# Segment-max pass of a four-layer graph network: the message transposes two chunks ahead, the scan one chunk ahead of the additions, three partial sums to a bank

## The reference, cut to what matters

```python
msgs = z[edge_dst] @ Wd + z[edge_src] @ Ws + edge_weight[:, None] * ww[None, :] + bm
agg = jax.ops.segment_max(msgs, edge_dst, num_segments=n)
...
agg = jnp.where(deg[:, None] > 0, agg, jnp.zeros((), dtype=z.dtype))
...
hidden = jax.nn.relu(z @ W1a + agg @ W1b + b1)
return hidden @ W2 + b2                      # then residual, layer norm, and the table of the last pass
```

## Time and profile before

| | |
|---|---|
| Median of 3 runs | 3425.28 us (3420.51 to 3431.15) |
| Profiled execution, span | 4033.3 us |
| Mean granted TensorE clock in it | 0.859 |
| Max pass in it (first to last scan) | 1997.7 to 3379.1 us |
| Busy share, whole span: PE, PEld, DVE, ACT, POOL | 80, 56, 42, 24, 59 % |

### The profile page before, as it was taken

One profiled execution on the slowest core, in us unless ns is written; L12 is line 12 of the kernel. 1 busy time (PEld: TensorE's weight loads), 2 busy tenths in 40 slices (PEclk: granted clock), 3 DMA queues, 4 the chain that ended last, 5 costly groups with the idle time before them and its releaser, 6 DMA issues.

```text
span 4033.3 us, 59669 instructions
## 1 busy us (share of the span) xinstructions
PE 3216.6 (80%) x22050; PEld 2272.7 (56%) x22050; DVE 1712.9 (42%) x3999; ACT 954.4 (24%) x2526; POOL 2364.2 (59%) x2341
## 2 busy tenths in 40 slices
PE   3688788788888888888677887777777786989898
PEld 2344444455557777776455665555665664545554
DVE  6465555132231222111355555555655564333333
ACT  2455455132230111011222222222222222000000
POOL 3766662666634666665255555655655562677775
PEclk6899999889999999998777678877877777999999
DMA  5444444656555666665432333333333335666564
GB/s 150 146 158 166 164 144 155 203 174 198 183 163 193 198 198 208 200 190 189 142 94 74 101 102 101 104 101 102 105 112 96 100 108 195 238 202 227 199 217 138
DMA packets 285336, 629.16 MB, mean 156 GB/s; under 512 B 60235, under 2 KB 194964, under 8 KB 277494
## 3 DMA queue, kind: packets, MB, share of 16 engines
q1 hardware_dynamic: 178038, 378.50, 27.5%
q0 software_dynamic: 105280, 245.39, 20.7%
q10 hardware_dynamic: 1728, 1.38, 0.1%
HBM read 480.93 MB, written 144.13 MB: 155 GB/s over the span
## 4 chain that ended last, share of the span: by engine, by line
PE 60%; issue 15%; another core or an unknown queue 8%; DVE 8%; ACT 6%; DMA 1%; DVEq 1%; SPq 0%; POOL 0%; ACTq 0%; POOLq 0%
PE banks L1777 25%; PE banks L1239 7%; PE banks L461 7%; PE banks L549 4%; PE banks L1798 3%; PE banks L1258 3%; PE banks L1796 3%; PE banks L1234 2%; PE banks L524 2%; PE banks L1893 1%; PE banks L1127 1%; ACT arena L2126 1%; DVE arena L488 1%; ACT arena L1409 1%
## 5 line engine op out<-in xcount | busy, mean ns | idle before, releaser
L1777 PE MATMUL banks<-arena 128*128 128x384 bf16 (+1 forms) x9310 | 1545.1, 315 | 123.8 <-issue 115.1
L1777 PEld LDWEIGHTS banks<-arena 128*128 128x128 bf16 x9310 | 910.6, 100 | 603.9 <-issue 218.4
L511 POOL DMA_INDIRECT arena<-tab_l,ring_of_rows x831 | 819.8, 986 | 615.6 <-PE banks L1239 330.6
L461 PE MATMUL banks<-arena 128*128 x1758 | 426.9, 352 | 321.1 <-issue 161.3
L1844 POOL DMA_INDIRECT arena<-h_pieces,span_sources x450 | 434.6, 966 | 315.0 <-issue 107.1
L1844 POOL DMA_INDIRECT ring_of_rows<-message_pieces,span_sources x396 | 429.4, 1084 | 227.2 <-issue 101.0
L461 PEld LDWEIGHTS banks<-arena 128*128 128x128 f32 x1758 | 331.7, 245 | 386.7 <-issue 385.4
L1822 DVE TENSOR_TENSOR arena<-iota_bf,span_targets 128x768 bf16<-128x768 bf16 x243 | 135.1, 557 | 837.1 <-remote 337.8
L488 DVE TENSOR_TENSOR arena<-arena,banks 128x129 f32 x879 | 251.6, 286 | 537.3 <-PE banks L461 337.9
L1844 POOL DMA_INDIRECT ring_of_rows<-x_pieces,span_sources x306 | 334.1, 1092 | 202.9 <-PE banks L1796 91.4
L1844 POOL DMA_INDIRECT ring_of_rows<-l_pieces,span_sources x306 | 300.0, 980 | 232.7 <-issue 71.9
(11 more groups left out here) (246 smaller groups left out, 3151.2 us busy)
## 6 DMA issues: line engine op xcount, KB each, us to landing
arena<-edge_counts SPq DMA_DIRECT2D x83, 896.0 KB
arena<-edge_counts SPq DMA_DIRECT2D x83, 672.0 KB
edge_counts<-arena SPq DMA_DIRECT2D x32, 1568.0 KB
typed_counts<-arena SPq DMA_DIRECT2D x27, 1568.0 KB
arena<-scan_mask SPq DMA_DIRECT2D x208, 128.0 KB
arena<-typed_counts SPq DMA_DIRECT2D x27, 896.0 KB
arena<-typed_counts SPq DMA_DIRECT2D x27, 672.0 KB
arena<-tab_l,ring_of_rows POOLq DMA_INDIRECT x831
```

Of the source, the lines that this page charges most:

```text
L461: T.matmul(place(s, k.bank[:n_banks], cols), k.OH[:, s % OH_RING, :], k.RG[:, bass.ds(base, cols)], start=True, stop=True).then_inc(p.prod ...
L511: k.nc.gpsimd.indirect_dma_start(k.RG3[:, i % p.ring, at:at + width], None, table, bass.IndirectOffsetOnAxis(ap=k.SRC[:, i:i + 1], axis=0) ...
L1777: t = T.matmul(k.bank[i % N_SUMS][:, 0:rows.shape[-1]], counts[:, s, :], rows, start=s == 0 and n == 0, stop=s == NT - 1 and n == len(term ...
```

## The change: what it does

It concerns the regular program's max pass.

- TensorE gets a function of its own, `max_tensor_l2`. Messages are turned two chunks ahead, alternately into banks 2 and 6. The order for chunk c is slot 0, `turn_messages(c + 2)`, slot 1, turn back c, slot 2, typed counts, slot 3.
- VectorE runs scan c + 1 ahead of chunk c's additions (`max_chunks`).
- Step results go three to a bank (`TRIPLE`, 136 columns each), still in banks 0 and 1. The lag of the additions stays at two steps (`MAX_LAG`). The first addition of three waits for all three products; products of a triple wait for the additions of the triple two before it.
- Masks and weight rows get a third buffer (`MASKS`).
- The dense part of a group uses one bank (`max_bank`) in place of four. The last projection and its bias addition are therefore done in two halves of two node tiles (`parts`, `table`, `parts2`, `table2`), which makes 21 stages of 19. The number of steps between stages (71 or 72 steps // stages) stays 3 for the full groups.
- Three semaphores are merged with others.

```diff
+MAX_LAG = 2
+TURNS_OF_MAX = (2, 6)
+MASKS = 3
+TRIPLE, TRIPLE_COLS = 3, 136
...
-    "l2": (*STAGES["l2"], *PIECES),
+    "l2": (*STAGES["l2"], "parts2", "table2", *PIECES),
...
+def max_bank(g):
+    return banks_of(g)[0]
+def max_tiles(g, half):
+    return gtiles(g)[2 * half:2 * half + 2]
...
+def max_place(k, s):
+    return k.bank[s // TRIPLE % 2][:, s % TRIPLE * TRIPLE_COLS:s % TRIPLE * TRIPLE_COLS + H + 1]
...
+    def step(s):
...
+        if s % OH_BATCH == 0:
+            T.wait_ge(p.hot, s // OH_BATCH + 1)
+        if s % TRIPLE == 0 and s >= 2 * TRIPLE:
+            T.wait_ge(p.added, s - TRIPLE)
+        if s == 0 or p.newest(s) // CH != p.newest(s - 1) // CH:
+            T.wait_ge(k.sem("l2_back_copied"), p.newest(s) // CH + 1)
+        T.matmul(max_place(k, s), k.OH[:, s % OH_RING, :], k.RG[:, bass.ds(base, H + 1)], start=True, stop=True).then_inc(p.product, 1)
...
+    def turn_messages(c):
+        tiles, bank = chunk_tiles(c), k.bank[TURNS_OF_MAX[c % 2]]
+        if c >= 2:
+            T.wait_ge(k.sem("l2_scanned"), c - 1)
...
+    turn_messages(0)
+    turn_messages(1)
+    T.wait_ge(k.sem("l2_acc_set"), 1)
+    for c in range(NCH):
+        steps(k.slots[c][0])
+        if c + 2 < NCH:
+            turn_messages(c + 2)
+        steps(k.slots[c][1])
+        turn_back(c)
+        steps(k.slots[c][2])
+        if typed_unit(c):
+            tensor_typed_counts(k, *typed_unit(c))
+        steps(k.slots[c][3])
...
+    def add(s):
+        if s % TRIPLE == 0:
+            V.wait_ge(p.product, min(s + TRIPLE, STEPS))
...
+    def scan(c):
+        n = len(chunk_tiles(c)) * P
+        V.wait_ge(k.sem("l2_turned"), c + 1)
+        V.wait_ge(k.sem(f"load_mask_{c % MASKS}"), 32 * (c // MASKS + 1))
+        if c >= 2:
+            V.wait_ge(k.sem("l2_back"), c - 1)
...
+    def max_chunks():
+        scan(0)
+        for c in range(NCH):
+            if c + 1 < NCH:
+                scan(c + 1)
+            for which in k.slots[c][0:3]:
+                steps(which)
...
```

More of the change, by code:

```diff
@@ L1227, in turn_messages @@
         tiles = chunk_tiles(c)
-        if not p.regular:
-            T.wait_ge(k.sem("l2_message"), tiles[-1] + 1)
+        T.wait_ge(k.sem("l2_message"), tiles[-1] + 1)
         if c:
             T.wait_ge(k.sem("l2_scanned"), c)
-        if p.regular:
-            T.wait_ge(k.sem(f"load_mask_{c % 2}"), 32 * (c // 2 + 1))
-            T.matmul(k.bank[TURN][:, 0:len(tiles) * P], k.WW9, k.W9[c % 2][:, 0:len(tiles) * P], start=True, stop=False)
         for q, i in enumerate(tiles):
[L1236 to L1241, removed]
+            t = T.transpose(k.bank[TURN][:, q * P:(q + 1) * P], k.RG3[:, i % p.ring, UP:UP + H], k.IDENT)
         t.then_inc(k.sem("l2_turned"), 1)
@@ L1292, in node @@
             vector_invert(k, p, g, stage)
+        elif stage in ("table", "table2") and p.regular:
+            half = stage == "table2"
+            if max_tiles(g, half):
+                V.wait_ge(*p.at("parts2" if half else "parts", g))
+                rows, n = wide(region(k.HT, g, H2), H2), len(max_tiles(g, half))
+                V.tensor_tensor(rows[:, 2 * half:2 * half + n, :], wide(k.bank[max_bank(g)][:, 0:n * H2], H2), spread(k.bdc, n, H2),
+                                ALU.add).then_inc(p.sem(stage), 1)
         elif stage == "table":
             V.wait_ge(*p.at("parts", g))
-            if before_group(g) >= 0 and not p.regular:
+            if before_group(g) >= 0:
                 V.wait_ge(*p.stored("l3", before_group(g)))
@@ L1311, in node, with max_step @@
             t.then_inc(p.sem(stage), 1)
+    def add(s):
+        if s % TRIPLE == 0:
+            V.wait_ge(p.product, min(s + TRIPLE, STEPS))
+        if s:
+            V.wait_ge(p.added, s)
+        if s % REGS == 0:
+            V.load(k.ve_regs, k.BASES[1:2, s:s + REGS])
+        dst = k.ACC[:, bass.ds(V.snap(k.ve_regs[s % REGS], min_val=0, max_val=(NT - 1) * SLOT), H + 1)]
+        V.tensor_tensor(dst, dst, max_place(k, s), ALU.add).then_inc(p.added, 1)
+    def max_step(s):
+        if s == 0:
+            vector_one_hots(k, p, 0, k.LOCEND)
+        if s % OH_BATCH == 0 and s + OH_BATCH < STEPS:
+            vector_one_hots(k, p, s + OH_BATCH, k.LOCEND)
+        if s >= MAX_LAG:
+            add(s - MAX_LAG)
@@ new lines, in max_chunks @@
+    def max_chunks():
[5 more added lines that the diff above has]
+                steps(which)
+            if typed_unit(c + 2) and c % 2 == 0:
+                vector_typed_one_hots(k, (c + 2 + UNITS) // 2)
+            if c in FIRST_TYPE_AT:
+                vector_first_type(k, Plan(k, "l3", True), 0, FIRST_TYPE_AT.index(c))
+            if c in FIRST_HOT_AT:
+                vector_rows_hot(k, Plan(k, "l3", True), FIRST_HOT_AT.index(c))
+            steps(k.slots[c][3])
+        steps(k.slots[NCH][0])
+        for s in range(STEPS - MAX_LAG, STEPS):
+            add(s)
+        for stage, g in p.tail:
+            node(stage, g)
@@ L1319, in message @@
     def message(i):
-        if i < N_ET and not p.regular:
+        if i < N_ET:
             V.wait_ge(*p.landed(i))
@@ L1470, in first_slab @@
         load_typed_slab(k, Plan(k, "l3", True), 0, h)
-    load_mask(0)
-    load_mask(1)
+    for c in range(masks):
+        load_mask(c)
     if p.regular:
@@ L1480, in sync_l2 @@
         typed_end(c)
[L1481 to L1482 removed]
+        if c + masks < NCH:
+            load_mask(c + masks)
         for which in k.slots[c]:
@@ L3437, in build @@
         k.WW9 = k.ww[0:9, 0:H // 2].bitcast(BF16)
-        k.W9 = [k.RING[0:9, N_ET + n * 256:N_ET + (n + 1) * 256].bitcast(BF16) for n in range(2)]
+        k.W9 = [k.RING[0:9, N_ET + n * 256:N_ET + (n + 1) * 256].bitcast(BF16) for n in range(MASKS)]
         k.regular_weights = (*((k.WW9[3 * n:3 * n + 3, :], k.row_parts_dram) for n in range(3)), *k.late_weights[1:])
```

119 lines of the change are left out of this document (88 added, 31 removed).

## The result

The changed kernel takes 3399.15 us (median of 5 runs, 3396.41 to 3401.48), the kernel before 3420.78 us in the same comparison. The ratio is 0.993, 95% interval 0.991 to 0.9949: 22 us faster, where 135 were forecast. The size was six times too large. The prediction gives two ranges: its own range of 3200 to 3380 us doesn't hold the time, the one it ends with, 3183 to 3410 us, does.

A forecast was written before the change was run, and what follows sets the result against it. It took a ring of waits in the max pass as the bound: 208 x (6.67 - 5.8) = 181 us, less 5, 176 us of 4033.3, scaled to 149 (3276), forecast 3290 us; own range 3200 to 3380, final 3183 to 3410.

The forecast's parts named there:

- ring of waits: Max pass: PE, DVE, POOL and ScalarE wait on each other, no engine full; 2.25 us of waits in a 6.03 us chunk.
- rival 1: Max pass: gathers bind already, POOL's 5.06 us a chunk leaves 52 us of gain, 3373 us; chance 0.19.
- From the profiled to the timed run: Whole kernel: 176 us of profiled gain scaled to 149 us of 3425, 3276 us; forecast set at 3290.
- signs I named for being right: Profile after: 208 scans in about 1200 us, copy waits under 30, POOL's under 100 us, clock 0.8 or more.
- Standstills of PE half absorbed: Max pass: half of the 0.57 us a chunk from PE's stands of several us absorbed, leaving 0.28.
- Turning two ahead, second bank: Max pass, PE's turns: removes PE's wait for the scan, 1.31 us in the chunk shown.
- Weights keep their slack: Max pass, mask and weight loads: issued and read in the same chunk as before, with a third buffer.
- Earlier turn back: Max pass, before slot 2: PE's 0.64 us copy wait shrinks to about 0.1 at full clock, nothing at half.
- Triples at 0: Max pass, three steps to a bank: cost taken as 0, between bounds of 0 and 440 us.
- Rival 3: First addition of each triple: no step of grace, 293 us lost against 181 gained, 3520 us; chance 0.10.
- DVE's floor of 4.65 us: Max pass: DVE needs 892 us over 192 chunks, 4.65 us per chunk, if it never waited.
- rival 2: Max pass: PE's clock comes back, all chunks at 5.3 us, 242 us scaled gain, 3183 us; chance 0.13.

The follow-up runs named there:

- e2: Kernel before with every other gather of the max pass left out (half of the gathers): 3399.29 us, ratio 0.993.
- e3: Changed kernel with every other gather of the max pass left out (half of the gathers): 3304.01 us, ratio 0.9649.
- e1: Kernel before, unedited, profiled a second time: 3417.62 us (one run), span 3413.6 us.
- e5: Changed kernel, all gathers, messages turned one chunk ahead in two banks, each scan at the head of its own chunk: 3399.24 us, ratio 0.9916.
- e7: Changed kernel, half of the gathers, messages turned one chunk ahead in two banks, scans at the head of their own chunk: 3292.17 us, ratio 0.9603.
- e12: Kernel before, all gathers, only the turn back moved ahead of slot 2 and the typed counts: 3431.21 us, ratio 1.0008.
- e9: e7 with the turn back put behind slot 2 and the typed counts again; half of the gathers: 3307.38 us, ratio 0.966.
- e4: Changed kernel, all gathers, two steps to a bank in place of three: 3397.66 us, ratio 0.9921.
- e6: Changed kernel, half of the gathers, two steps to a bank in place of three: 3307.49 us, ratio 0.9649.
- e10: e7 with one bank for turned messages, each turn waiting for the previous chunk's scan; half of the gathers: 3625.37 us, ratio 1.0591.
- e14: e13 with all the gathers, on the slower chip: 4028.18 us, ratio 0.9993.
- e13: e9 with pairs in place of triples and the turn behind slot 1; half of the gathers, on the slower chip: 3712.59 us, ratio 0.9199.
- e17: e13 run again away from the slower chip; half of the gathers: 3376.05 us, ratio 0.9872.
- e8: Changed kernel, all gathers, one-hots for the max pass's typed counts cut to two elements each: 3389.01 us, ratio 0.9886.

## Why the prediction was right in direction and wrong in size

- **The bound.** I wrote that the pass is a ring of waits and not a full engine. There was a ring, and e2 against e3 shows 95 us in it. It did lead e1's chain, but a second bound lay just under it: POOL, at 5.2 us of a chunk's 5.34, left 0.14 us. I had POOL's floor (5.06 us) and the true time of a chunk at full clock (5.35), side by side, and made them rival 1. Its mechanism is what happened, at 22 us in place of its 52. Most of that miss is in the floor: I divided POOL's 972 us by 192 chunks, but the 755 gathers in that window are 188.8 chunks' worth (they run ahead, and the last starts at 3353.5 us), which makes 5.15, and the mean gather is 1.00 us in place of that trace's 0.985. Measured it is 5.20.
- **The step that failed** is "From the profiled to the timed run". The term 208 x (6.67 - 5.8) starts from 6.67 us a chunk. In an execution like the timed ones it is 5.34 (e1), and 0.14 x 207 = 28 us was saved between first and last scan, 22 in the time. Of the 0.87 us only some 0.03 were a gain at full clock (5.35 to 5.3, for 60% of the chunks). The rest was stalls absorbed (0.3), chunks moved from half to full clock (0.3) and waits at half clock (0.2), and e1 hardly has the stalls and runs at a clock of 0.88 already. I saw that 608 us could not be placed and scaled the gain by 0.85 all the same. More than half of them, 343 us, lie outside the max pass (4033.3 - 1381.4 against 3413.6 - 1104.9). POOL's 311.6 us of waits, my argument against rival 1, were 22.1 us in e1. The signs I named for being right (waits for the copy under 30 us, POOL's under 100, clock at 0.8 or more) all came with the small gain: they could not tell my forecast from rival 1.
- **Standstills of PE half absorbed**: they are hardly there; PE's longest wait for a copy in e1 is 0.8 us. Chunks in the earlier trace rows with pieces of 8.4 and 9.8 us come from the other kind of execution.
- **Turning two ahead, second bank.** That the wait for the scan goes was right, but it was 8.5 us over the whole of e1's pass and not 1.31 us a chunk. The lead that I gave the gain to is a part that can go without loss (e5, e7). What counts is the bank, and with it the turn ahead of slot 1. My reading is that PE then issues the turn before it stops at slot 1's wait for additions; that is argued, not shown.
- **Weights keep their slack**: wrong. PE waits 28.2 us for them in ten pieces, and e3 has them too; in e1 it is 1.2 us beyond the first load. SyncE stores each group's messages in the same queue: it waits 82.1 us for them after against 21.2 us in e1, and PE is a chunk further on. The nine of these waits that are over 1 us each end 6 to 11 us after such a store is issued, which bears this out.

```profile
SPq L651 <- DVE zt L1412: 82.1, 11, 10.9
```

- **Earlier turn back.** The copy's wait went as predicted, and was worth nothing to the kernel before (e12); from e9 to e7 it is 15 us with overlapping intervals.
- **Triples at 0**: right, with all gathers (e4) and with half (e6). Rival 3, additions without a step of grace, did not come in the changed kernel: its additions wait 202.4 us for products against 200.7. Their waits in e10 are 316.5 us over 960 us; how much of that is the triples stays open.
- **DVE's floor of 4.65 us**: no run went under it; with half of the gathers the pass runs at 4.70 (e7) and 4.76 (e3). That VectorE is what holds it there isn't shown: its additions still wait 102.9 us for products in e7. A slip in rival 3: at 1.5 us each, 41% of the triples cancel the 181 us, not 45%.
- **Clock**: 0.88 to 0.89, no return of the clock, rival 2 is out. With half of the gathers it is higher in both kernels. Windows of e2, then of e3:

```profile
1720.00:2680.00 960.00, 789.04 (x5770) 613.73 (x5769) 711.53 (x1577) 308.99 (x680) 378.68 (x374) 0.91 0.36 105
```

```profile
1720.00:2680.00 960.00, 825.61 (x6256) 657.03 (x6255) 765.64 (x1717) 348.99 (x738) 403.53 (x402) 0.92 0.39 113
```

The clock is 0.91 with PE busy 82% and 0.92 with 86%, so PE's share of idle time hardly moves it here. By the Trainium skill's "HAM oscillation — how this bites in real kernels" section ("TensorE: Matmul & The Clock Gate"), idle gaps between bursts of matmuls drop PE to half clock. From e1 to the changed kernel PE stays as idle as before (busy 83% in both), since its waits moved to the landing of rows, so these runs neither bear the rule out nor speak against it.
- **The occupancy rule** of the Trainium skill ("Perfetto Trace Analysis", "Identifying the Most-Contended Engine"), which I had set aside, would have been the better guide on e1's profile: POOL is busy 74% against DVE's 72%, and the rest of POOL's time is the 0.30 us that belongs to each gather. The lead is narrow, and relieving POOL alone was worth no more than the change, 24 us (e2).
- Not tried: the price of the single bank for the dense part, which I put at 5 us.

## What to carry to other kernels

Before a gain is worked out from waits, work out each engine's time per unit with the gaps that belong to its instructions, and compare the largest with the measured period: the difference is all that a pipeline can give. Where the second bound is about as large as the first, taking either away alone gives next to nothing (here 22 and 24 us), and both together a lot (120). If the profiled execution is far from the timed runs, take another profile before any term is sized. To see what parts of a pipeline do, take the bound engine's work away first; behind the bound every part looks the same. Signs of being right should be such as the rivals don't share.

## What the runs showed of the hardware that was not expected

- On one chip every kernel was slower: 4041 us against 3424. Of its 620 us (spans of 4033 and 3414), 343 lie outside the max pass, 290 of them ahead of it (first scan at 1998 us in place of 1707). The loss within the pass goes with its gathers: with all of them it takes 1371 us (e14, first to last scan), with half 1065 us (e13), against 1054 us for the same kernel elsewhere (e17). PE's gaps over 2.5 us number some 80 in e14's whole trace, some 40 in e13's, and some 25 in e1's (but some 35 after the change). Why is open. In one of them in the trace of before (2146.9 to 2152.4 us) ScalarE's copy starts 5 us after PE's transposes have ended, released by nothing that the view names, while POOL gathers on.
- An indirect gather of 128 rows holds POOL 0.94 us at the median, up to 2.7 us (e1), and 0.30 us pass before the next in e1 and after the change (246.3 us behind 808 gathers). The mean over the median costs 47 us in the pass, 12 of which went with VectorE's bf16 comparisons (e8). In the changed kernel the 176 gathers that overlap such a comparison take 0.14 us over the median each, the other 655 take 0.03.
